# The first two chunks' projection, norm and transposes of a post-norm layer, placed inside the last two attention heads

## What is computed

```
x  = layernorm(x + attention(x) @ w_out + b_out)
x  = layernorm(x + (silu(x @ wg.T) * (x @ wu.T)) @ wd.T)
```

## Time and profile before

| | |
|---|---|
| median of 3 runs | 2902.68 us (2900.68 to 2911.16) |
| the profiled execution | 2904.76 us, its span 2902.9 us |
| TensorE busy, share of the span | 98% |
| VectorE | 94% |
| ScalarE | 89% |
| GpSimd | 30% |
| mean granted TensorE clock | 0.985 of full speed |

### The profile page before, as it was taken

How to read it: one execution, slowest core, us unless ns; L and a number is a source line. 1 busy time by engine, 2 the same in 40 slices (tenths; PEclk the granted TensorE clock), 3 DMA queues, 4 the chain that set the end, 5 groups by cost and what they waited for, 6 DMA issues and landing times. The chain is left out here.

```text
span 2902.9 us, 68160 instructions
## 1 busy us (share of the span) xinstructions
PE 2832.9 (98%) x27022; PEld 882.6 (30%) x27022; DVE 2731.3 (94%) x3144; ACT 2586.9 (89%) x4718; POOL 857.1 (30%) x2100
## 2 busy tenths in 40 slices
PE   8989999999999999999999999999999999979998
PEld 4532222222222222222222222222222222246665
DVE  7989999999999999999999999999999999657776
ACT  5746999999999999999999999999999999946555
POOL 7841222222222222222222222222222222236553
PEclk9978999999999999999999999999999999999999
DMA  5431111111111111111111111111111111223431
GB/s 192 148 108 29 35 35 35 35 35 35 35 35 35 35 35 35 35 35 35 35 35 35 35 35 35 35 35 35 35 35 35 35 35 35 57 79 99 117 95 37
DMA packets 120865, 145.89 MB, mean 50 GB/s; under 512 B 52576, under 2 KB 86752, under 8 KB 120544
## 3 DMA queue, kind: packets, MB, share of 16 engines
q1 hardware_dynamic: 120256, 141.51, 16.5%
q10 hardware_dynamic: 288, 0.01, 0.0%
HBM read 105.78 MB, written 35.13 MB: 49 GB/s over the span
## 5 line engine op out<-in xcount | busy, mean ns | idle before, releaser
L903 ACT ACTIVATE probs<-st_ps 128x512 f32<-128x512 f32 x4096 | 2217.0, 599 | 97.3 <-PE st_ps L812 46.4
L932 DVE TENSOR_REDUCE tile_max<-s_ps 128x1 f32<-128x1024 f32 (+1 forms) x2048 | 2300.6, 1194 | 1.7 <-PE s_ps L796 1.6
L823 PE MATMUL o_ps<-probs,kept_v 128*17 128x256 f32 x16384 | 1282.8, 385 | 22.6 <-ACT sums L884 22.6
L796 PE MATMUL s_ps<-k,q 64*128 64x512 f16 x4096 | 1252.3, 386 | 14.1 <-PEq L88 7.4
L812 PE MATMUL st_ps<-q,k 64*128 64x512 f16 x4096 | 1236.4, 382 | 0.0
L823 PEld LDWEIGHTS o_ps<-probs,kept_v 128*17 128x17 f32 x16384 | 273.7, 95 | 874.4 <-ACT probs L903 455.1
L812 PEld LDWEIGHTS st_ps<-q,k 64*128 64x128 f16 x4096 | 266.5, 93 | 874.9 <-ACT probs L903 840.5
L1018 POOL TENSOR_SCALAR max_scaled<-neg_max_t 128x32 f32<-128x32 f32 x64 | 18.7, 291 | 1655.8 <-DVE neg_max_t L947 1655.8
L796 PEld LDWEIGHTS s_ps<-k,q 64*128 64x128 f16 x4096 | 240.5, 94 | 54.4 <-DVE tile_max L932 43.1
L1035 POOL TENSOR_TENSOR larger<-spared 128x256 f32<-128x256 f32 x558 | 171.9, 308 | 39.0
L1044 POOL TENSOR_TENSOR spared<-spared,larger 128x256 f32<-128x256 f32 x496 | 159.7, 322 | 41.3
(11 more groups left out here) (106 smaller groups left out, 1492.4 us busy)
## 6 DMA issues: line engine op xcount, KB each, us to landing
q<-q_parts SPq DMA_DIRECT2D x192, 128.0 KB
k<-k_parts SPq DMA_DIRECT2D x192, 128.0 KB
x_t<-in_x_t SPq DMA_DIRECT2D x16, 512.0 KB, 7.8
q_parts<-parts SPq DMA_DIRECT2D x32, 256.0 KB, 2.6
k_parts<-parts SPq DMA_DIRECT2D x32, 256.0 KB, 2.6
heads_out<-sums SPq DMA_DIRECT2D x256, 32.0 KB, 2.0
kept_v<-heads_out SPq DMA_DIRECT2D x16, 512.0 KB, 6.0
kept_v<-inverses_out SPq DMA_DIRECT2D x32, 256.0 KB
```

What stands on the lines that cost most here:

```text
L796: mm = pe.matmul(s_ps[g % 2][:, j * BANK:(j + 1) * BANK], q[h % 2][FIRST, r // KW * P:(r // KW + 1) * P], k[h % 2][FIRST, at:at + BANK], s ...
L823: mm = pe.matmul(o_ps[c * 32:c * 32 + VM, at:at + HALF], t["kept"][:, h, kt, :], probs[(h * KT + kt) % RING][:, c * BANK + at:c * BANK + a ...
L903: act.activation(probs[(h * KT + kt) % RING][:, c * BANK:(c + 1) * BANK], st_ps[n % ST][:, :], ACT.Exp, scale=scale).then_inc(exp_done, 1)
L932: dve.tensor_reduce(tile_max[h % 2][:, r // KW, r % KW:r % KW + 1], s_ps[g % 2][:, own], AX.X, ALU.max).then_inc(s_read, 1)
```

## The change

The two projections move to single steps: chunk 0 to steps 25, 27, 29, 31 of head 62, chunk 1 to steps 1, 3, 5, 7 of head 63. VectorE takes the flags first, then halves the weights, adds and counts both chunks, and adds eps for both at once; one square root follows in ScalarE's stream after step 14 of head 63, one inversion, and both chunks are normalized. The flag's product stands in step 9, its copies behind step 11, chunk 0's transposes in steps 18 and 20, its high parts behind 20 and 22, its whole parts behind 25 and 27. SyncE issues the loads of chunks 0 and 1 after head 62's maxima (during head 61) and chunk 2's at the end of `attend`; GpSimd divides and biases chunks 0 and 1 before it cuts head 63's maxima, and chunk 2 at the end of `attend`. The Silu table is loaded at the end of `attend`. Tiles and semaphores that are now used in more than one block are made ahead of them: `x1_t`, `x1_high`, `x1_low`, `warm`, `tile_max`, and the two `s_ps`, which `project` uses as `qk_ps` and `finish` as `t_ps` and `p_ps`. From chunk 1 on, the work of `finish` keeps its order; the square roots are counted one lower.

```diff
--- before.py
+++ after.py
@@ -498,6 +506,7 @@
+    t_ps = s["s_ps"][0][:, :].rearrange("p (k n) -> p k n", k=KD)
...
+    def first_sums(dve, product):
+        z = [f["z"], f["x1"][1]]
+        for c in range(2):
+            dve.wait_ge(f["biased"], c + 1)
+            for j in range(2):
+                dve.wait_ge(f["proj_done"], 2 * c + j + 1)
+                dve.tensor_tensor(z[c][:, 2 * j:2 * j + 2, :], product[c][:, 2 * j:2 * j + 2, :],
+                                  f["x_in"][c][:, 2 * j:2 * j + 2, :], ALU.add).then_inc(f["z_done"], 1)
+            dve.wait_ge(f["z_done"], 2 * c + 2)
+            count(dve, z[c], TT * c, f["z_stats"])
+            average(dve, TT * c, c, f["z_stats"], f["z_moments"])
...
+    PROJECT_0 = (25, 27, 29, 31)
+    PROJECT_1 = (1, 3, 5, 7)
+    SUM_WIDE = 9
+    KEEP_WIDE = 11
+    DEVIATIONS = 14
+    TRANSPOSE_0 = (18, 20)
+    TAKE_HIGH = (20, 22)
+    TAKE_WHOLE = (25, 27)
...
@@ -765,18 +818,19 @@
                 if h + 2 < HEADS:
                     sp.wait_ge(s_done, (h + 1) * MAXES)
                     first_stacks(sp, t, s, h + 2)
-                if h == HEADS - 1:
+                if h > 0:
+                    out["keep"](sp, h - 1)
+                    out["inverses"](sp, h - 1)
+                if h + 1 < HEADS:
+                    maxima(h + 1)
+                if h == HEADS - 3:
                     sp.wait_ge(pv_done, OVERLAID * KT)
                     for i in range(2):
                         sp.wait_ge(kept[i], N_HEAD // 2 * QC * 16)
                         sp.wait_ge(inverses_out[i], N_HEAD // 2 * 16)
                     for c in range(2):
                         steps["load"](sp, c)
-                if h > 0:
-                    out["keep"](sp, h - 1)
-                    out["inverses"](sp, h - 1)
-                if h + 1 < HEADS:
-                    maxima(h + 1)
+            steps["load"](sp, 2)
...
+            def beside(h, n):
+                if h == HEADS - 2 and n in PROJECT_0:
+                    if n == PROJECT_0[0]:
+                        pe.wait_ge(s_read, TILES - 1)
+                    steps["output_projection"](pe, 0, p_first[0], [PROJECT_0.index(n)])
+                if h == HEADS - 1 and n in PROJECT_1:
+                    if n == PROJECT_1[0]:
+                        pe.wait_ge(s_read, TILES)
+                    steps["output_projection"](pe, 1, p_first[1], [PROJECT_1.index(n)])
+                if h == HEADS - 1 and n == SUM_WIDE:
+                    pe.wait_ge(topped, 2 * len(FFN) + 2)
+                    pe.wait_ge(f["z_done"], 2)
+                    pe.matmul(s_ps[0][:, 0:1], w["ones"][:, :], w["wide"][:, :], start=True, stop=True
+                              ).then_inc(f["wide_summed"], 1)
+                if h == HEADS - 1 and n in TRANSPOSE_0:
+                    if n == TRANSPOSE_0[0]:
+                        pe.wait_ge(f["x1_done"], 1)
+                        pe.wait_ge(f["wide_known"], 1)
+                    steps["transpose"](pe, 0, TRANSPOSE_0.index(n))
@@ -854,16 +929,9 @@
                     elif h > 0:
                         times_v(h - 1, KT + before, half)
                     scores_t(h, 2 * n + 1)
-                    if h == HEADS - 1 and n >= EXPS // 2 - 2 * TT:
-                        c, tile = divmod(n - EXPS // 2 + 2 * TT, TT)
-                        if tile == 0:
-                            pe.wait_ge(s_read, TILES - 1 + c)
-                        steps["output_projection"](pe, c, p_first[c], [tile])
+                    beside(h, n)
             for kt, half in ((KT - 2, 1), (KT - 1, 0), (KT - 1, 1)):
                 times_v(HEADS - 1, kt, half)
-            pe.wait_ge(topped, 2 * len(FFN) + 2)
-            pe.matmul(st_ps[0][:, 0:1], w["ones"][:, :], w["wide"][:, :], start=True, stop=True
-                      ).then_inc(f["wide_summed"], 1)
+            def beside(n):
+                if n == KEEP_WIDE:
+                    act.wait_ge(f["wide_summed"], 1)
+                    act.copy(f["wide_count"][:, :], s_ps[0][:, 0:1]).then_inc(f["wide_known"], 1)
+                    act.wait_ge(f["wide_known"], 1)
+                    act.copy(f["wide_int"][:, :], f["wide_count"][0:1, :]).then_inc(f["wide_known"], 1)
+                if n == DEVIATIONS:
+                    steps["deviations"](act, 0)
+                if n in TAKE_HIGH:
+                    steps["take_high"](act, 0, TAKE_HIGH.index(n))
+                if n in TAKE_WHOLE:
+                    steps["take_whole"](act, 0, TAKE_WHOLE.index(n))
@@ -907,13 +989,10 @@
                     g = (h + 1) * MAXES + LEAD + e // 2
                     if e % 2 == 0 and g in SPARED:
                         keep_half(SPARED.index(g))
+                    if h == HEADS - 1 and e % 2 == 1:
+                        beside(e // 2)
             drain(HEADS - 1)
-            for c in range(2):
-                steps["deviations"](act, c)
-            act.wait_ge(f["wide_summed"], 1)
-            act.copy(f["wide_count"][:, :], st_ps[0][:, 0:1]).then_inc(f["wide_known"], 1)
-            act.wait_ge(f["wide_known"], 1)
-            act.copy(f["wide_int"][:, :], f["wide_count"][0:1, :]).then_inc(f["wide_known"], 1)
+            steps["load_silu"](act)
@@ -982,19 +1061,18 @@
                         turn_maxima(g // MAXES - 1)
                     if n == 20 and h > 0:
                         out["invert"](dve, h - 1)
-                if h == HEADS - 1:
+                if h == HEADS - 2:
+                    flag_wide()
                     halve_weights()
-                    flag_wide()
-
-            dve.memset(f["moments"][:, :, :], 1.0).then_inc(f["z_moments"], 1)
+                    dve.memset(f["moments"][:, :, :], 1.0).then_inc(f["z_moments"], 1)
+                    dve.wait_ge(f["z_moments"], 1)
+                    steps["first_sums"](dve, p_first)
+                    steps["variances"](dve, 0, 2, 0)
+            steps["invert"](dve, 0, 0, 0)
             for c in range(2):
-                steps["sum_z"](dve, c, p_first[c])
-                steps["count_z"](dve, c)
-                steps["average_z"](dve, c)
-                steps["variances"](dve, c, c + 1, 0)
-                if c == 0:
-                    steps["invert"](dve, 0, 0, 0)
-                    steps["normalize"](dve, f["x1"][0], f["z"], 0, f["x1_done"])
+                steps["normalize"](dve, f["x1"][c], (f["z"], f["x1"][1])[c], TT * c, f["x1_done"])
+            for kd in range(KD):
+                steps["take_low"](dve, 0, kd)
@@ -1055,13 +1133,16 @@
                 cut(h)
                 if h + 1 < HEADS:
                     fold(h - 1)
-            pool.wait_ge(bias_added, 1)
-            for c in range(2):
-                steps["divide"](pool, c)
-                steps["bias"](pool, c)
+                if h == HEADS - 2:
+                    pool.wait_ge(bias_added, 1)
+                    for c in range(2):
+                        steps["divide"](pool, c)
+                        steps["bias"](pool, c)
+            steps["divide"](pool, 2)
+            steps["bias"](pool, 2)
...
@@ finish @@
-            steps["load"](sp, AHEAD)
             out["keep"](sp, HEADS - 1)
...
-            transpose(0)
             wide = pe.value_load(f["wide_int"][0:1, 0:1], min_val=0, max_val=P)
...
-            load_silu()
-            take_transposed(0)
...
-            low(0)
...
-            steps["divide"](pool, AHEAD)
-            steps["bias"](pool, AHEAD)
```

More of the change, by code:

```diff
@@ L471, in norm_state @@
         down_factor=sb("down_factor", [P, 1]),
+        x1_t=sb("x1_t", [P, KD, BANK]),
+        x1_high=sb("x1_high", [P, KD, BANK], F16),
+        x1_low=sb("x1_low", [P, KD, BANK], F16),
+        warm=sb("warm", [P, 1]),
+        turned=sem("turned"),
+        x1_high_done=sem("x1_high_done"),
+        x1_low_done=sem("x1_low_done"),
+        x1_t_done=sem("x1_t_done"),
         wide_summed=sem("wide_summed"),
@@ L565, in count_z, with transpose, take_high, take_low @@
         count(dve, f["z"], 0, f["z_stats"])
+    def first_sums(dve, product):
[9 more added lines that the diff above has]
+            average(dve, TT * c, c, f["z_stats"], f["z_moments"])
+    def transpose(pe, c, kd):
+        for n in range(TT):
+            mm = pe.transpose(t_ps[:, kd, n * P:(n + 1) * P], f["x1"][c % 2][:, n, kd * P:(kd + 1) * P],
+                              w["ident"][:, :])
+        mm.then_inc(f["turned"], 1)
+    def take_high(act, c, kd):
+        act.wait_ge(f["turned"], KD * c + kd + 1)
+        act.activation(f["x1_high"][:, kd, :], t_ps[:, kd, :], ACT.Copy, scale=X1_SCALE
+                       ).then_inc(f["x1_high_done"], 1)
+    def take_low(dve, c, kd):
+        dve.wait_ge(f["x1_high_done"], KD * c + kd + 1)
+        dve.scalar_tensor_tensor(f["x1_low"][:, kd, :], t_ps[:, kd, :], X1_SCALE, f["x1_high"][:, kd, :],
+                                 ALU.mult, ALU.subtract).then_inc(f["x1_low_done"], 1)
+    def take_whole(act, c, kd):
```

(20 more changed lines are left out.)

72 lines of the change are left out of this document (31 added, 41 removed).

## The result

The changed kernel takes 2912.74 us (median of 14 runs, 2911.08 to 2917.74), the kernel before 2905.35 on the same chips (14 runs): ratio 1.0028, interval 1.0022 to 1.0035. It is slower by 7 to 8 us; the forecast was 2899 and the range ended at 2908. The profiled execution has a span of 2912.0 us, 9.1 more than before.

What follows compares the result with a forecast made beforehand. TensorE and ScalarE were both taken as full in the last heads. Tail terms of -9.95 us and last-head terms of +6.0 gave -4.0, from the median 2902.7 a forecast of 2899 us, range 2892 to 2908.

Steps and rivals of the forecast that it cites:

- rival C: Last head: TensorE stops some 2 us at the root, its clock falls and stays down; +15 us, 2914; chance 0.05.
- (a): Tail: shorter chain behind the last product with V, so the new block starts 6.0 us earlier.
- (b): New block: no transposes ahead of flag load and branch; first FFN product 4.9 us from block start, gain 1.0.
- (c): Tail: chunk 2 divided and biased inside the last head, so TensorE's wait of 1.95 us goes.
- (d): Tail: chunk 0's down products wait less for GpSimd's `h_low`; gain 1.0 us, ends 0 and 1.4.
- The switch of tables: Last head, ScalarE: two table loads around the root at 1.28 us each, without the skill's 1.38 drain.
- ScalarE's copies and takes: Last head: two flag copies 0.37 us, two `x1_high` and two `x1_t` 2.42; 0.3 of ScalarE's added work taken as hidden.
- The transposes: Last head: eight on TensorE right behind the table loads, where it waits anyway; cost 0.3 us, ends 0 and 1.2.
- The projections: Eight output projections spread over the last two heads instead of one: 9.4 us before and after, change 0.
- Rival A: Last heads: ScalarE sets the pace, TensorE has slack, spaced projections partly hidden by 2.8 us; 2896; chance 0.15.
- Rival B: Last head: each stop of ScalarE loses 1.0 us more at restart, 3.0 in all; 2901.7; chance 0.10.
- Rival D: Last head: chunk 2's division on GpSimd slows chunk 0's normalization, TensorE waits at transposes; up to +4, 2903; chance 0.08.

Runs made afterwards that it cites:

- e3: The kernel before, plus one tiny square root with unused result on ScalarE behind step 14 of head 63: 2912.70 us, ratio 1.0034 to the kernel before.
- e4: The kernel before, plus one tiny square root with unused result on ScalarE behind step 10 of head 62: 2906.35 us, ratio 1.0007 to the kernel before.
- e5: e1 plus two ScalarE copies into unread scratch tiles behind step 14's second exponential: two levels, median 2904.79 us, ratio 1.0004 to the kernel before.
- e2: The changed kernel plus ten unread products on TensorE in step 16 of head 63, where it would stop: 2899.20 us, ratio 0.9984 to the kernel before.
- e6: e1 plus one ScalarE copy (128 x 1,152 values) into an unread tile behind step 14's second exponential: 2897.53 us, ratio 0.9981 to the kernel before.
- e1: The changed kernel with its first root made by VectorE, so ScalarE loads no table in head 63: 2897.23 us, ratio 0.9977 to the kernel before.
- e7: e1 with the flag loaded behind the last V products, only the branch left at the tail's start: 2895.99 us, ratio 0.9974 to the kernel before.
- e8: e7 plus nine unread products on TensorE behind the last V products: 2898.09 us, ratio 0.9983 to the kernel before.

## Why the prediction was wrong

**The step that failed** is the condition I gave rival C. Its mechanism, place and size were right, and it is what happened. I wrote that it "decides at a stop of TensorE as long as the one after the last product; it speaks against it that the stop is half of that", and gave it 0.05. The stop came as I had it, "some 2 us", and measured 2.26. But it needed no more: the clock fell in the profiles of after, e3 and e4 behind stops of 2.23 to 2.26 us, and in e5's behind one of 1.74. The earlier trace rows showed when the clock had fallen in one long idle time, and I read it as how long an idle time it takes. The fall in after came some 2 us after TensorE had already started again, so the two are not the same. The row showed a stop that was long enough, not the shortest that is, and "half of it" was no evidence against.

The trace of before has no stop of TensorE inside a head, but it has two of the length that I forecast elsewhere, and the prediction uses neither for C. In the first block TensorE waits 1.97 us, and by the 0.81 of its row the clock falls at about 22.5, 0.7 us after TensorE has started again. In the tail it waits 1.95 us for chunk 2's division, and the clock stays at 1.00:

```profile
21.81 0.35 PE L215 MATMUL v_ps<-bounds,ones_qk 128*128 128x3 f32 x2 [1.97 <-DVE bounds L329]
...
20.00:24.00 4.00, 2.19 (x5) 1.20 (x6) 3.90 (x9) 0.65 (x2) 0.00 (x0) 0.81 0.50 186
...
2582.00:2586.00 4.00, 2.90 (x13) 2.58 (x14) 4.00 (x4) 0.00 (x0) 3.41 (x2) 1.00 0.72 195
```

The stop in the first block is in all ten profiles. The clock fell behind it in six, each with 1.97 us, and stayed in four, with 1.97 (e5), 2.15 (e2) and 2.35 us (e3, e6). So at about 2 us the length of a stop does not decide alone. One fall and one stay in the trace that I had say that the chance should have been near even, and the range should have reached 2914.

The other half of C, "and stay down", I took without a reason, though the trace of before has the like at the start of the attention, where the clock stays at 0.50 from 184 to 244 us with TensorE at times busy for the whole of a row:

```profile
224.00:228.00 4.00, 4.00 (x9) 0.50 0.01 4
```

e3 and e4 show it for the last heads: after the same stop, steps with scores or projections lift the clock and plain steps don't. By after - e2 the clock cost 12.6 us in the stretch; I had 15. The difference is mostly the count of steps: I let all 18 behind the root run at the low clock, but it fell two steps behind the stop, and 14 were left, 14 x 0.85 = 11.9. The last 24 products with V lifted it, but only at about 2578.8 by the 0.90 in the row from 2578, 0.5 us before their end.

"HAM oscillation — how this bites in real kernels" in the Trainium skill's "TensorE: Matmul & The Clock Gate", which I named beside C, warns of gaps in TensorE's work that let its clock fall, but of longer ones than this. The 0.50 above, behind 2.26 us, agrees with it in kind and not in length, and here the measurement decides.

**The sum, term by term**, now with the clock kept (e2, e1) and as it ran (after):

- The ends of the sum: I wrote -11.3 + 4.9 for the lower one and left out the flag's 0.4, so it should read -11.3 + 5.3 = -6.0. Nothing else hangs on it.
- (a) and (b), the tail up to the first FFN product: forecast 7.0 us shorter, measured 14.52 - 7.34 = 7.2. From the new block's start, which the first issue of SyncE marks at 2581.72, it took 4.99 to that product; I had 4.9. Right. e7 adds that 1.3 of it is the load of the flag.
- (c) right: the projection starts without a wait. (d) right in kind: the down products follow each other at 0.11 us from 2604.22 in after. In e8 the first of them waited 1.39 us for `h_low`, so this wait is near to coming back.
- The tail in all: forecast -9.95, measured -10.4 in e2 and -8.7 in after. The tails of e1, e2, e6, e7 and e8, with the same work in them up to the flag's load, differ by 1.8 us, so I read no more into that.
- The switch of tables: forecast 2.8, measured 2.6 (e2 - e1). The second table starts 0.01 us behind the root, much as the first load in the earlier trace rows began 0.03 behind the copy. The Trainium skill's drain of 1.38 us ("ScalarE: Activation LUTs", section "What ACT_TABLE_LOAD costs") would have made it 5.3; it isn't seen here either.
- The rest of the last head, ScalarE's copies and takes, flag and transposes: forecast 5.3 - 2.8 + 0.4 + 0.3 = 3.2, measured 2.6 (81.35 - 78.72, in e1). The split was off. The transposes cost TensorE more than my 0.3, since in e1, with no stop for them to hide in, each of the two groups keeps its pair 0.7 us further apart, 1.4 in all and above my end of 1.2. With the flag's 0.4 that leaves about 0.8 for ScalarE's copies and takes, where I had 2.5. I had read its 3.98 of 4 as full, but in e1 fourteen exponentials with their inputs ready take 7.45 us, (7.45 - 0.60)/13 = 0.527 each, and the seven behind the root in after (3.54 - 0.60)/6 = 0.49. TensorE's step asks for 0.545. So ScalarE had slack, a few hundredths of a microsecond per exponential, and caught up between the takes.
- The projections: forecast 0, right. The step below, from the timeline of after, keeps its pair 1.38 us apart, as in the earlier trace rows, although the step behind it has no projection, and the pair behind that follows after 0.87 us (2510.76), as behind a projection in before. Rival A's hidden projections are refuted by it. ScalarE did not set the pace: the slack is ScalarE's.

```profile
2508.51 0.39 PE L866 MATMUL st_ps<-q,k 64*128 64x512 f16 x1
2508.82 1.13 PE L548 MATMUL s_ps<-w_out,kept_v 128*128 128x256 f32 x4
2509.89 0.39 PE L866 MATMUL st_ps<-q,k 64*128 64x512 f16 x1
```

- Rival B played no part that shows: without the clock's fall the head came out shorter than forecast. Rival D came close. I had chunk 2's load land 2 us behind the normalization of chunk 0; in after both chunks' normalization took 2.67 us for eight, and the division began 0.03 us behind its end, at 2547.00. In e2 the division began in its midst, at 2543.30, and the eight took 4.74 us; TensorE shows no wait for them at the transposes. That D cost nothing was in part luck.

Without the fall of the clock the sum would have held: e2, which is the change with the stop filled, came to 0.9984 (0.9974 to 0.9993); the forecast of -4.0 us is 0.9986. And the change is worth making if TensorE does not stop: e1 and e7 are faster than both kernels, e7 by 8.0 us against before and, as the two ratios to before stand, by about 16 against the change as it was.

What stays open: why the plain steps do not hold up the clock once it has fallen, although TensorE is 4.00 busy in them, and what besides its length decides whether a stop near 2 us is followed by the fall.

## What to carry to other kernels

Before a step is moved into a stretch where TensorE is full, ask whether it makes TensorE stop there, and what the work behind the stop is: the table loads that made it stop cost 2.6 us here, the clock that the stop brought down 12.6. If a stop can't be avoided, fill it with products that nobody reads, or put it where dense work follows (in head 62 the same stop lengthened the stretch by 3.7 us instead of 10.1). And where a risk rests on a condition, look through the whole trace for cases of it, outside the part that changes too; if it shows none or both outcomes, the chance is near even and the time belongs in the range.

## What the runs showed of the hardware that I had not expected

- In the last two heads a stop of 2.23 to 2.26 us was followed by the fall of TensorE's clock from 2.4 to 1.2 GHz in each of three profiles, one of 1.74 in one profile, and one of 0.36 us wasn't. In the first block a stop of 1.97 to 2.35 us was followed by it in six of ten profiles, and the longest were not among them. The fall came from 0 to 2.1 us after TensorE had started again.
- Once down, the clock stayed at 0.50 for some 30 us of plain steps and two groups of transposes (after), in which TensorE shows as 4.00 of 4 us busy. Steps with scores (e4), with projections (e3) and 24 products with V in a row (after) lifted it.
- A row of 0.60 us per exponential is a latency: with inputs ready they start every 0.49 to 0.53 us, so that ScalarE at 3.98 of 4 us had some slack.
- Ten products without a reader, put into a stop, cost nothing and kept the clock at 1.00 (e2); nine behind the last product, ahead of 3.90 us of idle time, brought nothing (e8).
- From the start of a block to its first product, with the load of a flag from SBUF into TensorE's register and a branch on it between them, it took 4.99 us (after); 1.3 of it goes when the load is made earlier (e7).
